# Queries and keys stored transposed and split ahead of each attention, with the value products moved between the two score products, in a two-layer transformer kernel

## The chip, the cores and the metric

The kernel runs on one core of one Trainium2 chip. The metric is device time in microseconds (us) of one execution, the median of three. Lower is better. The engines are TensorE (PE), VectorE (DVE), ScalarE (ACT), GpSimd (POOL) and SyncE (SP, which here only issues DMAs).

## The reference

```python
# x: 4 batches x 1024 tokens x 256 features, 16 heads of 16 features
x = x + ln(attn0(ln(x)))        # attn0: no mask, scores / sqrt(256)
x = x + ln(moe0(ln(x)))         # two loops of a routed MLP, 8 experts of 512
x = x + ln(attn1(ln(x)))        # attn1: causal, ALiBi slopes, biases on q, k, v, scores / sqrt(16)
x = moe1(x)                     # balanced assignment, 8 experts of 1024 (layer norm, gelu, residual)

def attn(x):
    q, k, v = split(x @ w_qkv (+ b_qkv))                # per head 16 features
    s = q @ k.T / scale (+ slope * (key_pos - query_pos), masked above the diagonal)
    return (softmax(s) @ v) @ w_out (+ b_out)
```

All of it is float32 and the output has to match to float32-like accuracy.

## The kernel before

The program is one sequence of stages, each with its own on-chip memory, its own semaphores and a barrier of all engines at its end: `ln_qkv` (layer norm and q, k, v), `attention` without mask, `attn_post`, twice `rms_logits`/`route`/`experts`, `combine_qkv` (the second layer's q, k, v), causal `attention`, `attn_post`, `assigned_experts`. Every engine has its own in-order instruction stream; semaphores tie them.

**The q, k, v stages.** `ln_qkv` and `combine_qkv` walk over 32 tiles of 128 tokens. For each tile TensorE transposes the normalised tokens (`turn`), then computes 768 outputs per token with the tokens on the partitions (`product`: a 512-wide and a 256-wide part, two contraction steps each; `combine_qkv` adds the bias by one more matmul per part). ScalarE copies the 768 columns out of PSUM (`y_out`) and stores them with one DMA of 384 KB in pieces of 64 floats, grouped by four heads (`qkv`).

**Attention.** It works on 32 pairs of heads. In `raw` lie the q, k, v of four heads with tokens on the partitions. A float32 number is split into a high part (rounded to what one fast `float32r` pass takes exactly) and the rest; q and k become rows of 64 columns per head: 5 columns for the row maximum and the positions, then 16 high, 16 high or rest, 16 rest or high. GpSimd builds these rows (`natural`), TensorE turns them (`fill`: four 128x128 transposes into the PSUM bank `TP`, four fills for a pair), ScalarE copies each half into `qT` or `kT` (`evac`). A `fill` and the transposes of the output (`finish`) share that bank, and the waits `t_bank_read` order them.

A pair is processed twice over: first the natural scores (queries on the partitions), of which VectorE takes the row maxima (`scores`, `rowmax`), then the transposed scores with the maximum subtracted (`qk`), of which ScalarE takes the exponential (`exp`), whose result goes into the value product (`pv`, four column groups for two steps at once). The maxima of one pair run beside the exponentials of the pair before. One pair is a *slot* of NS steps: 16 without mask, 12 with it. Each step issues, on TensorE in this order, `qk(n)`, then the natural scores of the step (`scores`, called m(n) below: the unit `max_at(n)`, four units ahead), then in odd steps `pv`. All scores live in a ring of three PSUM buffers (`s_free`), in the order e(0), m(0), e(1), m(1), ...; so `qk(n)` waits until VectorE has finished the maxima of step n-2, and `scores` of step n waits until ScalarE has finished `exp(n-1)`:

```python
ring={}
for n in range(NS):
    ring["e",n]=len(ring)%3
    if max_at(n)[0] is not None: ring["m",max_at(n)[0]]=len(ring)%3
    if n==TURN: ring["t",0]=len(ring)%3
```

At `TURN` (step 12, or 8 with the mask) the maxima of a pair are complete: VectorE reduces them (`mfinal`), TensorE turns them, VectorE copies them (`mcopy`) and SP writes them as one row of `qT` (`place`), which `qk(0)` of the next slot awaits. At step 4 and again at step 12 (without the mask) `finish` turns the output of one half and VectorE sums and scales it (`add`, `scale`).

The SP stream of attention: the loads of the first heads, in the first attention then the weights for the MLP stages (`ahead`), then the loop with loads, `place`, `store`.

## Time and profile before

| | us |
|---|---|
| three runs | 3403.23, 3406.68, 3409.97; median 3406.68 |
| the profiled execution, its own time | 3403.33 |
| span of its trace, first to last instruction | 3401.6 |

| stretch of the span | us | what runs there |
|---|---|---|
| 0 to 108 | 108 | `ln_qkv` |
| 108 to 1015 | 907 | attention without mask, begin of `attn_post` |
| 1015 to 1990 | 975 | `attn_post`, MLP of the first layer |
| 1990 to 2130 | 140 | `combine_qkv` |
| 2130 to 2815 | 685 | causal attention |
| 2815 to 3401 | 586 | `attn_post`, MLP of the second layer |

Busy shares over the span: PE 80%, DVE 58%, ACT 48%, POOL 28%. How to read it: a wait only costs where it lies on the chain that sets the end of its stage, so each stage has to be read by itself, in the timeline of its engines.

### The profile page before, as it was taken

The page shows a single profiled execution, that of the slowest core. Times are in us where ns is not written, and L with a number is a line of the kernel's source. Part 1 is how long each engine was busy: PE and PEld are TensorE (multiplying, and loading weights), DVE is VectorE, ACT ScalarE, POOL GpSimd, SP SyncE. Part 2 cuts the span into 40 slices and gives each one's busy share as a digit, 9 for nine tenths or more (in the row PEclk, how much of TensorE's full clock was granted, in tenths as well). Part 3 has the DMA queues.
Part 4 walks back from the last instruction along what each step waited for, and adds up shares of the span by engine and source line. Part 5 has one row for each costly group of instructions (what it writes and reads, how often), then busy time and mean ns, then how long its engine had stood idle before and what let it go on. Part 6 is the DMA issues. An engine that isn't in the chain of part 4 may idle for free. (4 is left out here: it accounts for less than half of the span.)

```text
span 3401.6 us, 63393 instructions
## 1 busy us (share of the span) xinstructions
PE 2729.3 (80%) x16332; PEld 1619.0 (48%) x16333; DVE 1966.6 (58%) x4600; ACT 1625.9 (48%) x2553; POOL 959.6 (28%) x1653
## 2 busy tenths in 40 slices
PE   8699999999977449995399959688888887718887
PEld 5333333333324438874388724344444444415554
DVE  3488888888845353335533354576667754556641
ACT  3277777777754433333333334366666663302212
POOL 1411111111126115541155444322222213403333
PEclk9699999999995569995599979799999996759999
DMA  6501010010013102214022166111111104322331
GB/s 168 168 20 24 14 25 19 19 25 13 19 40 113 56 16 69 68 58 149 14 69 68 59 174 183 44 26 25 31 26 30 25 10 121 119 92 70 99 100 61
DMA packets 365685, 215.08 MB, mean 63 GB/s; under 512 B 284782, under 2 KB 345842, under 8 KB 364791
## 3 DMA queue, kind: packets, MB, share of 16 engines
q1 hardware_dynamic: 231224, 106.71, 11.8%
q10 hardware_dynamic: 116416, 54.53, 5.5%
q0 software_dynamic: 17920, 52.46, 4.9%
q8 instruction: 43, 0.70, 0.1%
q14 instruction: 82, 0.67, 0.1%
HBM read 129.20 MB, written 85.98 MB: 63 GB/s over the span
## 5 line engine op out<-in xcount | busy, mean ns | idle before, releaser
L339 ACT ACTIVATE att_pr<-att_S 128x1024 f32<-128x1024 f32 (+1 forms) x896 | 836.1, 941 | 427.5 <-ACTq L346 424.4
L379 DVE TENSOR_REDUCE att_mparts<-att_S 128x2 f32<-128x1024 f32 x640 | 777.1, 1225 | 169.1 <-DVEq L375 165.2
L255 PE MATMUL att_S<-att_qT,att_kT 64*128 64x512 f32 (+3 forms) x1792 | 430.0, 472 | 46.4 <-PEq L250 42.1
L271 PE MATMUL att_OP<-att_pr,att_vn 128*32 128x512 f32 (+3 forms) x3584 | 451.1, 564 | 1.0 <-PEq L265 0.7
L243 PE MATMUL att_S<-att_kT,att_qT 64*128 64x512 f32 (+3 forms) x1792 | 391.0, 430 | 74.1 <-PEq L237 62.7
L255 PEld LDWEIGHTS att_S<-att_qT,att_kT 64*128 64x128 f32 x1792 | 175.0, 184 | 471.9 <-issue 460.7
L179 POOL COPY att_vn<-att_raw 128x256 f32<-128x256 f32 x64 | 25.4, 396 | 1148.6 <-POOLq L178 1148.6
L243 PEld LDWEIGHTS att_S<-att_kT,att_qT 64*128 64x128 f32 x1792 | 188.0, 190 | 173.0 <-issue 167.1
L385 DVE CUSTOM_DVE_ANT_0 att_unused<-att_S,att_mask 128x128 f32<-128x128 f32 (+3 forms) x512 | 228.3, 488 | 69.9 <-DVEq L375 69.9
L1067 POOL DMA_INDIRECT experts_xs<-scaled,ffn_source x144 | 140.2, 974 | 353.2 <-SPq L1060 163.5
L1164 DVE COPY experts_y<-experts_Y 128x256 f32<-128x256 f32 x144 | 61.2, 425 | 223.3 <-DVEq L1163 223.3
L1138 ACT ACTIVATE experts_hh<-experts_TH 128x512 fp32r<-128x512 f32 x144 | 86.2, 598 | 204.2 <-ACTq L1137 202.7
L1073 POOL DMA_INDIRECT mixed<-experts_y,ffn_target x144 | 146.2, 1016 | 92.5 <-issue 43.1
L1161 DVE TENSOR_TENSOR experts_hl<-experts_TH,experts_hh 128x512 fp32r<-128x512 f32 x144 | 99.6, 692 | 111.8 <-DVEq L1159 111.0
L1141 ACT ACTIVATE experts_h<-experts_H 128x512 f32<-128x512 f32 x144 | 86.2, 599 | 127.5 <-ACTq L1140 127.5
L1406 PE MATMUL ffn_Y<-ffn_w,ffn_hT 128*128 128x256 f32 x512 | 128.5, 402 | 8.9 <-PEq L1405 8.9
L1401 PE MATMUL ffn_H<-ffn_xT,ffn_w 128*128 128x512 f32 x256 | 121.1, 630 | 13.4 <-PEq L1399 9.1
L479 POOL TENSOR_TENSOR post_s<-post_s,post_half 128x2 f32<-128x2 f32 x128 | 97.1, 758 | 115.3 <-POOLq L651 109.1
L675 PE MATMUL post_Y<-post_w,post_aT 128*128 128x256 f32 x256 | 107.2, 563 | 27.8 <-PEq L673 27.8
L271 PEld LDWEIGHTS att_OP<-att_pr,att_vn 128*32 128x32 f32 x3584 | 72.0, 108 | 109.7 <-issue 105.3
L336 ACT ACTIVATE att_qT<-att_TP 128x512 fp32r<-128x512 f32 x128 | 76.1, 594 | 90.5 <-ACTq L334 90.5
L1406 PEld LDWEIGHTS ffn_Y<-ffn_w,ffn_hT 128*128 128x128 f32 x512 | 97.1, 198 | 33.7 <-issue 20.8
(291 smaller groups left out, 4913.0 us busy)
## 6 DMA issues: line engine op xcount, KB each, us to landing
qkv<-qkv_y ACTq DMA_DIRECT2D x64, 384.0 KB, 3.4
att_raw<-qkv SPq DMA_DIRECT2D x96, 256.0 KB, 3.3
rows<-post_rows ACTq DMA_DIRECT2D x32, 384.0 KB, 2.7
ffn_w<-in_w ACTq DMA_DIRECT2D x12, 1024.0 KB
ao<-att_aon SPq DMA_DIRECT2D x32, 256.0 KB, 2.8
post_at<-ao SPq DMA_DIRECT2D x64, 128.0 KB, 3.1
scaled<-rms_zs SPq DMA_DIRECT2D x64, 128.0 KB, 1.7
rms_rows<-mixed SPq DMA_DIRECT2D x32, 256.0 KB, 3.6
```

The costliest lines, as they stand in the source:

```text
L243: mm=pe.matmul(S[:,b,h,at:at+n],qT[r,s,qt*128:qt*128+128],kT[r,s,half*512:half*512+n],start=True,stop=True)
L255: mm=pe.matmul(S[:,b,h,f:512],kT[r,s,kt*128:kt*128+128],qT[r,s,c*512+f:c*512+512],start=True,stop=not diag)
L271: mm=pe.matmul(OP[32*j:32*j+32,f:512],vn[:,s,kt,h,:],pr[:,n%4,h,f:512],start=kt<2,stop=g in last_groups,skip_group_check=True)
L339: nc.scalar.activation(pr[:,n%4,:,f:512],S[:,ring["e",n],:,f:512],ACT.Exp,scale=exp_scale).then_inc(s_free[ring["e",n]],1)
L379: nc.vector.tensor_reduce(mparts[:,s,:,2*qt+half],S[:,b,:,0:width(qt,half)],AX.X,ALU.max).then_inc(end,1)
L385: nc.vector.tensor_tensor_reduce(unused[:,2*i+h,0:n],S[:,b,h,at:at+n],mask[:,512-n:512],1.0,-3.0e38,ALU.add,ALU.max,mparts[:,s,h,2*qt+half ...
L675: mm=pe.matmul(Y[:,u%4,0:DIM],aT[:,u%2,128*k:128*k+128],w[:,k,:],start=k==0,stop=k==KC-1 and not last)
L1067: nc.gpsimd.indirect_dma_start(out=xs[:,t%R,:],out_offset=None,in_=zs_d,in_offset=bass.IndirectOffsetOnAxis(ap=source[:,t:t+1],axis=0)).th ...
L1073: nc.gpsimd.indirect_dma_start(out=y2_d,out_offset=bass.IndirectOffsetOnAxis(ap=target[:,t:t+1],axis=0),in_=y[:,t%RY,:],in_offset=None, bo ...
L1161: V.tensor_tensor(hl[:,u%2],TH[:,u%2,:],hh[:,u%2].bitcast(F32),ALU.subtract).then_inc(hT_ready,1)
L1401: mm=pe.matmul(H[:,c%2,:],w1[:,e%2,k,128*c:128*c+128],xT[:,k,:],start=k==0,stop=k==KC-1)
L1406: if c<FC: pe.matmul(Y[:,t%2,0:DIM],hT[:,c,128*t:128*t+128],w2[:,e%2,c,:],start=c==0,stop=False)
```

## The change

Queries and keys are no longer stored with tokens on the partitions. `ln_qkv` and `combine_qkv` compute them with the features on the partitions (`features`: one block of 128 features by 512 tokens per step), ScalarE writes the high part (`high`, with the bias in the second layer), VectorE the rest (`low`), and SP stores both parts (`keep_block`, 512 KB); v is computed and stored alone (`values`, `v_out`, `keep_v`, 128 KB). The stages' steps are delayed against each other by whole tiles (`lagged`), and the loops over the tiles are written out. In attention, `natural`, `fill`, `evac` and the identity in `float32r` are gone; SP loads the parts into the rows of `qT` and `kT` directly, 14 or 16 DMAs of at most 64 KB per pair, into four sets instead of two. The constant rows are cleared or set at the start, for `kT` on VectorE. In a step, TensorE now issues `qk(n)`, in odd steps `pv`, then the natural scores.

```diff
 # attention, SP
+                def load_set(b,pair):
+                    s=pair%SETS; done=set_loaded[s]
+                    sp.wait_ge(set_free,1).then_inc(set_free,-1)
+                    for m,T,high,both in ((0,qT,AUG,AUG+HD),(1,kT,AUG+2*HD,AUG)):
+                        for h in range(2):
+                            to=lambda row,n: T[64*h+row:64*h+row+n,s,:].bitcast(F32)
+                            parts=qk_d[m][:,bass.ds(b*HEADS+2*pair+h,1)].bitcast(F32)
+                            sp.dma_start(to(high,HD),parts[0,0]).then_inc(done,16)
+                            for x in range(2): sp.dma_start(to(both+HD*x,HD),parts[x,0]).then_inc(done,16)
+                            if causal: sp.dma_start(to(0,AUG),augr[...,m,:].bitcast(F32)).then_inc(done,16)
+                            elif m==0: sp.dma_start(to(0,1),zeros[:].bitcast(F32)).then_inc(done,16)
+                def during(b,c,first,last):
+                    if not (last and c+3>=COUPLES): load_set(*later(c+3))
+                    if c%2==0: ...   # store of the group before, load_v of the next
+                    if not (last and c+1>=COUPLES): place(c+1)
+                for c in range(3): load_set(0,c)
+                load_v(0,0)
                 if ahead:
                     for k in range(KC): sp.dma_start(w1[:,k,:].bitcast(F32),...).then_inc(w_loaded[k],16)
...
+                place(0)
 # attention, GpSimd: natural() is removed, values() stays
+                pool.wait_ge(keys_cleared,2+causal).then_inc(keys_cleared,-2-causal)
+                pool.sem_inc(set_free,SETS); pool.sem_inc(rv_free,1)
 # attention, TensorE
                     for n in range(NS):
                         if e is not None: qk(e,n)
                         x,ahead=max_at(n)
-                        if m is not None and n==0: t_bank_read()
-                        if a is not None and n==NS-EARLY: t_bank_read()
                         s=a if ahead else m
                         unit=x is not None and s is not None
+                        g=(n-2)//2 if n>1 else GROUPS_PV-1
+                        who=prev if n<2 else e
+                        if who is not None and n%2==1:
+                            if g in (0,CHUNK0): o_ready(g,e,prev)
+                            pv(who,g)
                         if unit: scores(s,x)
                         if m is not None and n==TURN: turn_max()
-                        if m is not None and n==0: fill(m,0,1)
-                        ...   # four fills in all, removed
-                        g=(n-2)//2 if n>1 else GROUPS_PV-1
-                        who=prev if n<2 else e
-                        if who is not None:
-                            if n%2==0 and not unit: exp_read(2*g+1)
-                            if n%2==1:
-                                if g in (0,CHUNK0): o_ready(g,e,prev)
-                                pv(who,g)
+                        if prev is not None and n==2: pe.sem_inc(set_free,1)
+                        if who is not None and n%2==0 and not unit: exp_read(2*g+1)
                         if prev is not None and n==4: finish()
-                        if e is not None and n==KEYS0+1: finish()
+                        if e is not None and n==ADD0: finish()     # ADD0=NS-EARLY
 # attention, ScalarE: evac() and its four calls per slot are removed
 # attention, VectorE
+                nc.vector.memset(kT[:].bitcast(F32),0.0).then_inc(dve_done,1)     # 128 x 4*1024
                 nc.vector.memset(mparts[:],-3.0e38).then_inc(dve_done,1)
+                for h in range(2): nc.vector.memset(kT[64*h:64*h+1].bitcast(F32),-1.0).then_inc(keys_cleared,1)
                 if causal:
+                    nc.vector.tensor_copy(augr[:],augf[:]).then_inc(keys_cleared,1)   # 80 x 2048
 # ln_qkv (combine_qkv likewise, with its bias and longer lags)
+def lagged(stages):
+    for n in range(NT+max(lag for lag,stage in stages)):
+        for lag,stage in stages:
+            if 0<=n-lag<NT: stage(n-lag)
+                lagged(((0,load),(11,keep_v),(15,keep_block)))      # SP; combine_qkv: keep_v 14, keep_block 18
+                def features(q):                                    # TensorE
+                    f=q%4
+                    pe.wait_ge(q_free,1).then_inc(q_free,-1)
+                    for k in range(KC):
+                        mm=pe.matmul(Q[:,q%4],w[:,k,128*f:128*f+128],xT[:,k,q//4%2,:],start=k==0,stop=k==KC-1)
+                    mm.then_inc(q_full,1)
+                lagged(((5,values),(3,turn),(8,features)))          # combine_qkv: 8, 6, 11
+                def high(q):                                        # ScalarE
+                    act.wait_ge(q_full,1)...; act.wait_ge(hl_stored[q%HB],16)...
+                    nc.scalar.activation(hl[:,q%HB,0],Q[:,q%4],ACT.Copy).then_inc(high_ready,1)
+                lagged(((9,high),(4,turned),(7,v_given),(6,v_out)))
+                def low(q):                                         # VectorE
+                    dve.wait_ge(high_ready,1).then_inc(high_ready,-1)
+                    done(nc.vector.tensor_tensor(hl[:,q%HB,1],Q[:,q%4],hl[:,q%HB,0].bitcast(F32),ALU.subtract))
+                    dve.sem_inc(q_free,1); dve.sem_inc(low_ready,1)
+                lagged(((2,normal),(0,x_stats),(10,low)))
```

In `combine_qkv` the bias of q and k goes into `high` and `low`; v keeps its bias matmul, 256 wide. The outputs of the two layouts are the same numbers.

## Rows read from the trace of the kernel before

**Rows 1.** Stretches: length, busy us by engine, granted clock, DMA share, GB/s

```profile
108.00:1015.00 907.00, 790.56 (x4918) 318.42 (x4918) 686.31 (x779) 612.66 (x711) 160.82 (x313) 0.96 0.12 32
...
2130.00:2815.00 685.00, 583.08 (x4896) 315.87 (x4896) 457.07 (x1410) 405.74 (x576) 141.49 (x356) 0.97 0.12 26
```

**Rows 2.** Timeline, first attention: start, duration, engine, line, operation, idle before

```profile
525.45 0.49 PE L255 MATMUL att_S<-att_qT,att_kT 64*128 64x512 f32 x2
...
526.08 1.03 ACT L339 ACTIVATE att_pr<-att_S 128x1024 f32<-128x1024 f32 x1 [0.39 <-ACTq L346]
...
527.25 0.50 PE L243 MATMUL att_S<-att_kT,att_qT 64*128 64x512 f32 x2
...
527.68 1.06 PE L271 MATMUL att_OP<-att_pr,att_vn 128*32 128x512 f32 x8
527.90 1.23 DVE L379 TENSOR_REDUCE att_mparts<-att_S 128x2 f32<-128x1024 f32 x1 [0.18 <-DVEq L375]
...
528.67 0.50 PE L255 MATMUL att_S<-att_qT,att_kT 64*128 64x512 f32 x2
```

**Rows 3.** Timeline, first attention: transposed scores released by a maximum

```profile
508.31 1.23 DVE L379 TENSOR_REDUCE att_mparts<-att_S 128x2 f32<-128x1024 f32 x1
...
509.68 0.50 PE L255 MATMUL att_S<-att_qT,att_kT 64*128 64x512 f32 x2 [0.18 <-PEq L250]
```

**Rows 4.** Timeline, first attention: m(11), and `qk(13)` behind the turn

```profile
517.11 0.49 PE L243 MATMUL att_S<-att_kT,att_qT 64*128 64x512 f32 x2 [0.26 <-PEq L237]
...
520.38 0.50 PE L255 MATMUL att_S<-att_qT,att_kT 64*128 64x512 f32 x2
```

**Rows 5.** Timeline, causal attention: two turns, and the output transposes between them

```profile
2403.84 0.27 PE L285 MATMUL att_S<-att_ident,att_m 128*16 128x128 f32 x1
...
2418.36 0.63 PE L279 MATMUL att_TP<-att_ident,att_ot 128*128 128x128 f32 x4 [1.08 <-PEq L221]
...
2423.97 0.27 PE L285 MATMUL att_S<-att_ident,att_m 128*16 128x128 f32 x1 [0.15 <-PEq L284]
```

**Rows 6.** Timeline, start of the first attention

```profile
109.20 1.80 POOL L147 MEMSET att_qn<- 128x2048 f32 x1 [16.87 <-POOLq L29]
...
116.14 1.38 SPq L135 DMA_DIRECT2D ffn_w<-in_w  x2
...
126.74 0.80 PE L243 MATMUL att_S<-att_kT,att_qT 64*128 64x512 f32 x2 [1.02 <-PEq L237]
...
135.31 5.72 SPq L114 DMA_DIRECT2D att_raw<-qkv  x2
...
149.33 1.49 SPq L121 DMA_DIRECT2D att_qT<-att_mT  x2
...
152.50 0.79 PE L255 MATMUL att_S<-att_qT,att_kT 64*128 64x512 f32 x2 [0.82 <-PEq L250]
```

**Rows 7.** Timeline, start of the causal attention: two DMA issues of SP

```profile
2131.92 1.01 SPq L114 DMA_DIRECT2D att_raw<-qkv  x2
```

**Rows 8.** Instructions on `qkv_y`: min/median/max ns, first and last start

```profile
L599 ACT ACTIVATE qkv_y<-qkv_Y x32: 811/811/812, 16.7 to 104.0; 128x768 f32<-128x768 f32 x32
...
L1259 ACT ACTIVATE qkv_y<-qkv_Y x32: 811/812/812, 2001.0 to 2121.6; 128x768 f32<-128x768 f32 x32
```

**Rows 9.** Stretches of `ln_qkv`, weight loading and `combine_qkv`, columns as in Rows 1

```profile
20.00:40.00 20.00, 20.00 (x71) 11.87 (x70) 8.54 (x29) 8.55 (x15) 3.84 (x7) 1.00 0.77 187
...
116.00:126.00 10.00, 1.45 (x8) 1.13 (x8) 0.00 (x0) 0.75 (x2) 6.08 (x15) 0.50 1.12 378
...
2020.00:2040.00 20.00, 20.00 (x64) 9.91 (x64) 12.70 (x37) 11.03 (x21) 12.52 (x32) 1.00 0.94 239
```

**Rows 10.** Timeline, `ln_qkv`: the statistics of two tiles in a row

```profile
9.32 0.43 DVE L538 BATCH_NORM_STATS2 qkv_st<-qkv_xt 128x6 f32<-128x256 f32 x1 [0.44 <-DVEq L553]
...
11.34 0.43 DVE L538 BATCH_NORM_STATS2 qkv_st<-qkv_xt 128x6 f32<-128x256 f32 x1 [0.44 <-DVEq L553]
```

**Rows 11.** Groups by line: a 512-wide split on VectorE

```profile
L1161 DVE TENSOR_TENSOR experts_hl<-experts_TH,experts_hh 128x512 fp32r<-128x512 f32 x144 | 99.6, 692 | 111.8 <-DVEq L1159 111.0 <-ACT experts_hh L1138 0.7
```

More of the change, by code:

```diff
@@ L285, in turn_max, with slot, set_of @@
                     pe.transpose(S[0:2*TILES,b,0,0:128],m16[:],ident[:]).then_inc(mt_full,1)
-                def slot(e,prev,m,after):
-                    a=None if not after else 1-m
+                def slot(j,first,count):
+                    def set_of(ahead): return (j+ahead)%SETS if 0<=first+j+ahead<count else None
+                    e,prev,m,a=set_of(0),set_of(-1),set_of(1),set_of(2)
                     for n in range(NS):
@@ L604, in _, with v_out @@
-                pipelined(act,[turned,y_out])
-                if bias is None:
-                    for i in range(2): act.wait_ge(stored[i],16)
+                    nc.scalar.activation(xT[:,:,t//4%2,128*(t%4):128*(t%4)+128],T[:,t%2,0:DIM].rearrange("p (k c) -> p k c",k=KC),ACT.Copy).then_inc(xT_ready,1)
+                def v_out(t):
+                    act.wait_ge(v_full,1).then_inc(v_full,-1); act.wait_ge(v_stored[t%2],16).then_inc(v_stored[t%2],-16)
+                    nc.scalar.activation(v[:,t%2],V[:,t%2,0:DIM],ACT.Copy).then_inc(v_done,1)
@@ L608, in attn_post @@
+                for i in range(HB): act.wait_ge(hl_stored[i],16)
 def attn_post(nc,tag,ao,w_d,x_in,ident_d,x_out=None,z=None,bias_d=None,g_d=None,b_d=None,cent_d=None,rows_d=None,scores=None):
@@ L1277, in _ @@
-                done(V.tensor_copy(high[:],bias[:]))
-                done(V.tensor_tensor(low[:],bias[:],high[:].bitcast(F32),ALU.subtract))
-                done(V.tensor_scalar(low[:],low[:],ident[0:2,1:2],None,ALU.mult))
-                done(V.scalar_tensor_tensor(out=biasr[:],in0=high[:].bitcast(F32),scalar=ident[0:2,0:1],in1=low[:],op0=ALU.mult,op1=ALU.add))
+                done(V_.memset(ones[:].bitcast(F32),1.0))
+                done(V_.tensor_copy(split[:],bias[:]))
+                done(V_.tensor_tensor(rest[:],bias[:],split[:].bitcast(F32),ALU.subtract))
@@ L1281, in _ @@
+                done(V_.tensor_scalar(rest[:],rest[:],ident[0:2,1:2],None,ALU.mult))
+                done(V_.scalar_tensor_tensor(out=biasr[:],in0=split[:].bitcast(F32),scalar=ident[0:2,0:1],in1=rest[:],op0=ALU.mult,op1=ALU.add))
                 dve.sem_inc(bias_ready,1)
                 dve.sem_inc(rows_free,RR)
-                def weighted(s,b,u):
-                    V.scalar_tensor_tensor(out=row(z,b,u),in0=rows[:,u%RR,s],scalar=weight[:,s,bass.ds(b*TILES+u,1)],in1=row(z,b,u),op0=ALU.mult,op1=ALU.add).then_inc(dve_done,1)
```

496 lines of the change are left out of this document (204 added, 292 removed).

## The prediction

> **What bounds the kernel now.** I read the stretches first, then the timeline inside each stage that the change touches, because the busy shares alone don't say which wait ends last. The two attentions take 907 and 685 us of the span [rows 1]; PE is busy 87% and 85% of them, DVE 76% and 67%, ACT about 60%, and the granted clock is 0.96 and 0.97, that is 2.4 GHz nearly throughout. No engine is full, so the chain through them counts.
>
> In the first attention it closes every two steps [rows 2]. I write qk(n) for the transposed scores, m(n) for the natural scores of the same step. With the start of qk(even) at 525.45, its exponential starts at 526.08 (0.63 later) and takes 1.03; then m(odd) may overwrite that buffer, at 527.25 (0.14 after the end); `pv` follows at 527.68 (0.43); the next qk(even) starts at 528.67 (0.99). The sum is 0.63+1.03+0.14+0.43+0.99 = 3.22 us, and 528.67-525.45 is 3.22. The reader is to see that `pv` stands inside this loop, that the fills and ScalarE's copies mostly stand beside it, and that m(odd) waits for an exponential while PE idles.
>
> A second loop lies just beneath. m(odd) at 527.25 starts its maximum at 527.90 (0.65), which takes 1.23 and releases qk of the odd step after: 509.68 is 0.14 after the end of the maximum that began at 508.31 [rows 3]. From there to m(odd) another 0.43 or less: 0.65+1.23+0.14+0.4 = 2.4, hidden under 3.22 as long as `pv` is not in it.
>
> **The first attention.** The reorder takes `pv` out of the first loop and puts it into the second. PE's order becomes qk(even), m(even), qk(odd), pv, m(odd). qk(odd) still has to wait for the maximum of the last m(odd), `pv` is behind it in the queue, and m(odd) behind `pv`. The new loop is m(odd) to its maximum 0.65, maximum 1.23, release 0.14 [rows 3], qk(odd) to `pv` 0.43 (from m(odd) to `pv` now, the same shape), `pv` to m(odd) 0.99 (from `pv` to qk now): 3.44 us in place of 3.22. The old chain, without `pv`, is no longer the bound: exp(even) ends while `pv` runs. VectorE does its even maximum and the sums of the output (under 1 us at steps 4 and 12) inside the 3.44, which has room for 3.44-2x1.23 = 0.98.
>
> One pair of steps differs, where the row maxima are turned. From m(11) at 517.11 to qk(13) at 520.38 is 3.27 [rows 4], set by maximum, final reduce, turn and `finish`, none of which changes. Then m(13) comes 0.43+0.99 = 1.42 behind qk(13): 4.69. A slot is 7x3.44+4.69 = 28.8 us. For the slot before I take 7x3.22, and 3.27 plus 0.41 for m(13) directly behind qk(13), which is 26.2, and the stray 0.3 that the fills and copies add: 26.5 (from qk(0) at 152.50 [rows 6] to 1015, less some 13 for the last output and the next stage's start, over 32 slots, gives 26.5 too). So +2.3 per slot; the removal of fills and copies is already in it, worth only those 0.3. 32 slots x 2.2 (to stay with measured links) = **+71 us**. If every link were 0.05 shorter it would be +10, if VectorE lost its slack at steps 4 and 12 another +20.
>
> **The causal attention.** A slot is 20.13 us (2423.97-2403.84 [rows 5]) and VectorE runs nearly without a break. Two things pull. `finish` at 2418.36 waited 1.08 us for the shared bank that a fill held; that goes, and VectorE gets its sum about 0.5 us earlier. Against it, between m(1) and m(3) lie two full-width maxima, so the loop of 3.44 holds there while VectorE has only 2.46 of work: it idles 0.98. Between the other odd steps the maxima are narrow or masked and `pv` of the diagonal is shorter; following the same links I find 0.1 us lost before m(1) and 0.4 at step 9. The sum is -0.5-0.2+0.98+0.1+0.4 = +0.8 per slot, x32 = **+26 us** (bounds -0.5 and +2 per slot: -16 and +64).
>
> **Starts of the attentions.** No DMA of q and k may start before `kT` is cleared on VectorE: 128x4096, then twice one row of 4096. The trace has no such memset on VectorE; the nearest is 128x2048 on POOL, 1.80 us [rows 6], so 3.6 each and 10.8 for three, with 0 (if one row is cheap) to 21 as bounds. The Trainium skill (VectorE: DVE Perf Modes, "Zero memsets can be issued as uint32") says a memset takes one cycle per element, an estimate of 4.3 us each at 0.96 GHz, 12.8 for three; that would add 2 us per attention to the sum; no run here shows it yet. Then 14 DMAs at 0.5 us of issue each (1.01 for two [rows 7]) and some 2.3 to land (1.7 from the end of `place`'s issue to qk(0) [rows 6] is the nearest row): first natural scores at 109.2+10.8+7+2.3 = 129.3 instead of 126.74 [rows 6]. The larger delay is `place(0)`. SP now issues the loads of three pairs (42x0.5 = 21 us, until 141), then the weights, which took it from 116.14 to 135.31, 19.2 us [rows 6], and only then `place(0)`, at 161. Now it is issued at 149.33 and qk(0) starts 3.17 later, at 152.50 [rows 6]. So qk(0) at 164: **+11.5 us**. The causal attention has no such weights; with 10.8 of memsets, 1.8 for the position rows (2048 wide, by the same row), 8 of issue and 2.3 it starts its scores about **+5 us** later. GpSimd's building of rows, most of its 161 us in 907 [rows 1], goes too, from beside the path; its own waits hide it.
>
> **The q, k, v stages.** `ln_qkv` runs at (104.0-16.7)/31 = 2.82 us per tile, `combine_qkv` at 120.6/31 = 3.89 [rows 8], PE busy all of the time [rows 9]. PE's work in `ln_qkv` stays: as many columns, 1536 per tile. VectorE at its own pace took 2.02 per tile [rows 10]; `low` adds 0.69 [rows 11] and its waits, about 0.25: 2.97, now above PE's 2.82. The first ten steps run at 2.02, so only some 22 tiles pay 0.15 (+3), and the delayed steps leave a tail of five feature blocks and two value tiles, 10 us, before the last split is stored, where PE also idled at the start: about +1. Sum **+4 us**. In `combine_qkv` the 512-wide bias matmul goes. What that stage has over the other is 1.07 per tile for 768 columns of bias; two thirds would be 0.71, nothing is the other bound, and I take 0.43, what 512 columns take before `pv` [rows 2]: PE 3.46; VectorE, busy 12.70 of 20 us [rows 9], so 2.46 per tile, plus waits 0.4 and `low` 0.69: 3.6. That is -0.25 per tile, and a longer tail of 3: **-5 us**. DMA: per tile 640 KB are stored in pieces of 1 and 2 KB instead of 384 KB in pieces of 256 bytes. `ln_qkv` would move 0.79 MB per 2.97 us, 265 GB/s; `combine_qkv` 1.18 MB per 3.6, 328. The trace has 187 GB/s at a DMA share of 0.77 and 239 at 0.94, 243 to 254 at a full share, with 256-byte pieces, and 378 at 1.12, 337, with large ones [rows 9]. At the lower rate the stages would take 3.2 and 4.6 per tile, +8 and +24 us more; at the upper it hides. I take the upper, since the pieces are long.
>
> **Sum**, against the execution's own 3403.33 (span 3401.6): +71+26+11.5+5+4-5 = +112, so 3516; the median of the runs is 3.4 us above the profiled one, so **3519**.
>
> **Rivals.** (A) *The released loop wins, the time falls.* If qk(odd) doesn't wait for the odd maximum in practice, because that maximum starts early enough, what is left is VectorE's own work: 16x1.23 = 19.7, 1.7 of reduces and sums (686.31/32 less 19.7 [rows 1]) and as much again of waits, 23.2 per slot, -3.3x32 = -106 us in the first attention and -0.5x32 = -16 in the second, with +20 for starts and stages: 3305. It decides from the point where maximum plus release plus the link to `pv` is under 1.4 us instead of the 1.8 that rows 2 and 3 give. For it: DVE is idle a quarter of the time [rows 1] and PE idles before m(odd). Against: 0.14 at 509.68 is a wait on exactly that maximum [rows 3]. 13%. (B) *The loops even out*: the 0.22 is made up by links that shorten and by the missing fills; only starts and stages stay: 3403+16 to +40, 3430. 17%. (C) *The clock falls.* PE's work per two steps is four score pairs of at most 0.43 and `pv` 0.99, 2.7 of 3.44 us (79%), against the same and the fills in 3.22 (84% and more) [rows 2]. At the start of the attention, with maxima alone, the clock was at its lower level: the same pair of matmuls took 0.80 [rows 6] instead of 0.50 [rows 2]. Were it so in a third of the slots, the links 0.43 and 0.99 would double there, +1.42 per two steps, 11x8x1.42 = +125 over the forecast: 3645. The Trainium skill (TensorE: Matmul & The Clock Gate, the section on the transpose mode) says transposes don't count as busy the same way; by it the fills that go never held the clock, which makes C less likely; nothing here shows it apart. 6%. (D) *DMA-bound stages* on top of the forecast: +32, 3551; inside the forecast's range.
>
> **Numbers.** Forecast (with D) 64%, own range 3475 to 3575. Rival A 13%, B 17%, C 6%. The range of 8 in 10 has to reach into B: 3412 to 3585. What a measurement can tell from no change is about 0.2%, 7 us. Faster 0.15 (A, and a little of B), within 0.2% 0.03, slower 0.82.
>
> **What would show it.** Right: in the first attention the transposed scores of odd steps start 0.14 after a maximum, `pv` follows at 0.43, m(odd) 0.99 after; two steps take 3.44, a slot near 28.8; VectorE has a gap of about 1 us before each odd maximum; ScalarE's copies are gone and its waits have grown by more than that; qk(0) of the first attention starts some 11 us later behind the weights' issues. Wrong: VectorE's maxima back to back, a slot under 26.5, or `pv` starting before the maximum is done; a clock below 0.9 in the attentions; q, k, v stages over 3.2 and 4 us per tile with a DMA share near 1.

## The result, and the profile after

The changed kernel takes 3622.17 us (median of 4 runs, 3614.42 to 3628.47), the one before 3408.32 in the same runs: ratio 1.0628, 95% interval 1.0603 to 1.0653. The direction was as forecast, the size was twice as large: +214 instead of +112, above the range. The profiled execution has a span of 3626.7 us, 225.1 more than before, and they lie here (from first and last starts in the two traces; a stage begins with its first DMA issue, "steps" runs from the first qk to the last one of an attention):

| stretch | before | after | measured | forecast |
|---|---|---|---|---|
| `ln_qkv`, up to the first attention's start | 109.2 | 135.6 | +26.4 | +4 |
| first attention, start to qk(0) | 43.3 | 62.1 | +18.8 | +11.5 |
| first attention, steps | 840.4 | 950.0 | +109.6 | +71 |
| last qk to the causal attention's start | 1134.0 | 1157.4 | +23.4 | -5 |
| causal attention, start to qk(0) | 38.8 | 46.1 | +7.3 | +5 |
| causal attention, steps | 643.5 | 678.4 | +34.9 | +26 |
| rest | 592.4 | 597.1 | +4.7 | 0 |

`combine_qkv` alone grew by 23.7, from 162.5 to 186.2 us. The stretches of the changed kernel, in the columns of [rows 1]: they are longer by 129 and 42 us, PE's work is smaller, VectorE's is within 8 us of what it was, and the granted clock is 0.91 and 0.92 instead of 0.96 and 0.97.

```profile
134.00:1170.00 1036.00, 717.14 (x4406) 275.55 (x4406) 685.57 (x780) 565.11 (x582) 46.02 (x55) 0.91 0.16 45
2308.00:3035.00 727.00, 553.80 (x4384) 286.68 (x4384) 464.19 (x1414) 343.69 (x448) 14.38 (x35) 0.92 0.20 52
```

The timeline of the first attention, which answers [rows 2, 3] (L221 transposed scores, L209 natural scores, L237 `pv`, L325 maxima):

```profile
573.31 0.49 PE L221 MATMUL att_S<-att_qT,att_kT 64*128 64x512 f32 x2 [1.06 <-PEq L216]
573.73 1.07 PE L237 MATMUL att_OP<-att_pr,att_vn 128*32 128x512 f32 x8
...
574.73 0.50 PE L209 MATMUL att_S<-att_kT,att_qT 64*128 64x512 f32 x2
...
575.38 2.36 DVE L325 TENSOR_REDUCE att_mparts<-att_S 128x2 f32<-128x1024 f32 x2 [1.09 <-DVEq L321]
...
576.75 0.49 PE L221 MATMUL att_S<-att_qT,att_kT 64*128 64x512 f32 x2 [1.06 <-PEq L216]
```

This is the forecast loop, link by link: 0.42, 1.00, 0.65, then 1.37 for the maximum and its release; 3.44 us from 573.31 to 576.75. PE waits 1.06 and VectorE 1.09 in each round.

The turn, a few microseconds later, was not in the forecast (L250 the transposition of the maxima, L245 the output transposes):

```profile
578.17 0.50 PE L209 MATMUL att_S<-att_kT,att_qT 64*128 64x512 f32 x2
...
578.75 0.39 PE L209 MATMUL att_S<-att_kT,att_qT 64*128 64x512 f32 x2
580.77 0.27 PE L250 MATMUL att_S<-att_ident,att_m 128*16 128x128 f32 x1 [1.64 <-PEq L249]
580.93 0.63 PE L245 MATMUL att_TP<-att_ident,att_ot 128*128 128x128 f32 x4
581.48 0.80 PE L221 MATMUL att_S<-att_qT,att_kT 64*128 64x512 f32 x2
582.21 1.93 PE L237 MATMUL att_OP<-att_pr,att_vn 128*32 128x512 f32 x8
584.07 0.79 PE L209 MATMUL att_S<-att_kT,att_qT 64*128 64x512 f32 x2
```

PE has been idle for 1.64 us, and behind it the same products take 0.80, 1.93 and 0.79 instead of 0.49, 1.07 and 0.50: the granted clock has gone from 2.4 to 1.2 GHz. Before, PE waited 0.45 us ahead of the turn (median of 31 turns; now 1.64). The record of the granted clock has 24 stretches at the lower level in the steps of the first attention, 107 us in all; before there was one, of 10 us, right at their beginning.

`ln_qkv` (L522 the value product, L515 the transposition, L528 a feature block, L544 ScalarE's copy of it):

```profile
69.69 0.60 ACT L544 ACTIVATE qkv_hl<-qkv_Q 128x512 fp32r<-128x512 f32 x1 [2.48 <-ACTq L543]
...
70.06 1.10 PE L522 MATMUL qkv_V<-qkv_w,qkv_xT 128*128 128x256 f32 x4 [0.59 <-PEq L520]
...
71.00 0.38 PE L515 MATMUL qkv_T<-qkv_ident,qkv_xn 128*128 128x128 f32 x2
71.22 1.88 PE L528 MATMUL qkv_Q<-qkv_xT,qkv_w 128*128 128x512 f32 x4
...
73.32 0.60 ACT L544 ACTIVATE qkv_hl<-qkv_Q 128x512 fp32r<-128x512 f32 x1 [2.48 <-ACTq L543]
...
73.69 1.10 PE L522 MATMUL qkv_V<-qkv_w,qkv_xT 128*128 128x256 f32 x4 [0.59 <-PEq L520]
```

A step takes 3.63 us (forecast 2.97). PE waits 0.59 in these, at L520, the wait for a free bank of values, while ScalarE itself waits 2.48. In `combine_qkv` most steps take 4.41, and PE waits 0.91 at the same place.

The start of the first attention, which answers [rows 6]:

```profile
136.55 3.47 DVE L309 MEMSET att_kT<- 128x4096 f32 x1 [6.43 <-PEq L29]
...
141.12 3.47 DVE L312 MEMSET att_kT<- 1x4096 f32 x1 [1.02 <-DVEq L311]
...
145.50 3.47 DVE L312 MEMSET att_kT<- 1x4096 f32 x1 [0.91 <-issue]
...
180.62 0.27 DVE L354 CAST att_mT<-att_S 16x128 fp32r<-16x128 f32 x1
...
190.22 1.49 SPq L127 DMA_DIRECT2D att_qT<-att_mT  x2
...
197.72 0.80 PE L221 MATMUL att_S<-att_qT,att_kT 64*128 64x512 f32 x2 [15.22 <-PEq L216]
```

One memset takes 3.47 us, a memset of one row as long as that of the whole tile (forecast 3.6, from the row of GpSimd). The 4.3 estimated from the Trainium skill (VectorE: DVE Perf Modes, "Zero memsets can be issued as uint32") was too long for one; the measurement decides. But the three with the waits between them took 12.4 us, from 136.55 to 148.97. The maxima are ready at 180.9, but their placing waits in SP's queue until 190.22 behind the weights, and it now takes 6.0 us from the end of its issue to qk(0), not 1.7.

### The profile page after: what moved, and what is told of

It is laid out like the page before. It is cut to its first block and busy times, and to the rows that moved or that the text cites. A ratio compares the mean times of both kernels' runs of the same rounds, so it can differ in the third digit from the quotient of the medians.

```text
span 3626.7 us, 61395 instructions
## 1 busy us (share of the span) xinstructions
PE 2617.5 (72%) x15276; PEld 1537.2 (42%) x15277; DVE 2015.4 (56%) x4669; ACT 1518.0 (42%) x2361; POOL 716.3 (20%) x1074
## 5 line engine op out<-in xcount | busy, mean ns | idle before, releaser
L325 DVE TENSOR_REDUCE att_mparts<-att_S 128x2 f32<-128x1024 f32 x640 | 765.0, 1222 | 337.8 <-DVEq L321 336.4
L221 PE MATMUL att_S<-att_qT,att_kT 64*128 64x512 f32 (+3 forms) x1792 | 411.8, 448 | 348.9 <-PEq L216 346.5
L237 PE MATMUL att_OP<-att_pr,att_vn 128*32 128x512 f32 (+3 forms) x3584 | 484.5, 603 | 0.9 <-PEq L231 0.7
L209 PE MATMUL att_S<-att_kT,att_qT 64*128 64x512 f32 (+3 forms) x1792 | 411.4, 459 | 85.2 <-PEq L203 83.9
L221 PEld LDWEIGHTS att_S<-att_qT,att_kT 64*128 64x128 f32 x1792 | 192.1, 194 | 550.4 <-issue 547.1
L209 PEld LDWEIGHTS att_S<-att_kT,att_qT 64*128 64x128 f32 x1792 | 189.2, 199 | 456.9 <-issue 440.8
L1108 DVE COPY experts_y<-experts_Y 128x256 f32<-128x256 f32 x144 | 61.1, 425 | 225.1 <-DVEq L1107 225.1
L237 PEld LDWEIGHTS att_OP<-att_pr,att_vn 128*32 128x32 f32 x3584 | 72.9, 110 | 95.5 <-issue 84.3
L1033 PE MATMUL experts_H<-ffn_w1h,experts_xh 128*128 x288 | 104.7, 445 | 4.0 <-PEq L1041 3.1
```

Source lines behind the costliest of these rows:

```text
L209: mm=pe.matmul(S[:,b,h,at:at+n],qT[r,s,qt*128:qt*128+128],kT[r,s,half*512:half*512+n],start=True,stop=True)
L221: mm=pe.matmul(S[:,b,h,f:512],kT[r,s,kt*128:kt*128+128],qT[r,s,c*512+f:c*512+512],start=True,stop=not diag)
L237: mm=pe.matmul(OP[32*j:32*j+32,f:512],vn[:,s%2,kt,h,:],pr[:,n%4,h,f:512],start=kt<2,stop=g in last_groups,skip_group_check=True)
L325: nc.vector.tensor_reduce(mparts[:,s,:,2*qt+half],S[:,b,:,0:width(qt,half)],AX.X,ALU.max).then_inc(end,1)
L1033: mm=pe.matmul(out,a[:,128*k:128*k+128],b[:,k,bass.ds(at,width)],start=start and n==0 and k==0,stop=stop and n==len(pairs)-1 and k==chunks-1)
```

## The experiments

Each kernel ran in 3 rounds beside the kernel before, whose median was 3403.32 us for e1 to e4, 3408.19 for e5 to e8 and 3403.32 for e9 to e12. Stretches as in the table above, one profiled execution each; "low" is the time at the lower clock within the steps of an attention, of which 4 to 23 us at the head of each stand in every kernel. "Slot" runs from one transposition of the maxima to the next: the mean of the slots that ran wholly at the higher clock, and in brackets how many of the 30 had some time at the lower one. The edits are shown shortened.

| kernel | us | ln | start 1 | steps 1 | mid | start 2 | steps 2 | low 1 | low 2 | slot 1 | slot 2 |
|---|---|---|---|---|---|---|---|---|---|---|---|
| before | 3408.3 | 109.2 | 43.3 | 840.4 | 1134.0 | 38.8 | 643.5 | 10 | 7 | 26.52 (0) | 20.37 (1) |
| after | 3622.2 | 135.6 | 62.1 | 950.0 | 1157.4 | 46.1 | 678.4 | 107 | 70 | 28.92 (22) | 20.84 (13) |
| e1_pv_back | 3465.7 | 135.7 | 62.5 | 838.8 | 1153.3 | 46.1 | 625.1 | 13 | 30 | 26.44 (0) | 19.52 (7) |
| e2_before_pv_moved | 3517.8 | 109.9 | 43.4 | 927.7 | 1132.3 | 38.8 | 671.7 | 48 | 11 | 28.87 (11) | 21.20 (0) |
| e3_pv_early | 3529.8 | 135.5 | 61.8 | 875.8 | 1155.2 | 46.0 | 660.1 | 11 | 39 | 27.42 (0) | 20.41 (1) |
| e4_given_first | 3576.9 | 117.8 | 62.1 | 946.9 | 1127.0 | 46.1 | 686.5 | 101 | 98 | 29.00 (18) | 20.88 (16) |
| e5_pv_halves | 3479.2 | 135.4 | 62.3 | 821.0 | 1154.5 | 46.1 | 665.4 | 37 | 118 | 24.97 (5) | 19.93 (16) |
| e6_finish_first | 3589.6 | 135.9 | 62.0 | 907.3 | 1157.3 | 46.0 | 690.3 | 21 | 119 | 28.58 (0) | 20.77 (16) |
| e7_gap_filled | 3661.5 | 136.1 | 62.6 | 919.9 | 1161.1 | 46.1 | 735.8 | 8 | 92 | 29.08 (0) | 22.17 (21) |
| e8_starts | 3603.7 | 135.9 | 40.5 | 946.0 | 1160.4 | 41.2 | 687.3 | 94 | 107 | 28.98 (20) | 20.79 (17) |
| e9_mixed | 3384.9 | 117.7 | 40.6 | 827.7 | 1124.1 | 40.5 | 636.9 | 45 | 76 | 24.98 (6) | 19.45 (18) |
| e10_all_back | 3402.5 | 117.6 | 40.5 | 841.4 | 1125.3 | 41.2 | 642.9 | 12 | 100 | 26.45 (1) | 19.36 (26) |
| e11_before_halves | 3437.9 | 109.8 | 43.3 | 874.4 | 1128.1 | 38.8 | 643.2 | 4 | 10 | 27.61 (0) | 20.33 (0) |
| e12_gap_transposes | 3594.0 | 135.7 | 62.3 | 913.4 | 1152.3 | 46.0 | 694.1 | 9 | 129 | 28.90 (0) | 20.80 (17) |

In the changed kernel the slots of the first attention without a fall of the clock take 28.92 us and the 22 with one 30.50, so that the falls cost 22x1.58 = 35 us there. In the causal one it is 20.84 and 22.22: 13x1.38 = 18 us. The slots without a fall are the steadier measure: kernels with the same order in an attention agree in them to 0.2 us.

### The place of `pv`

**e1_pv_back**, on the changed kernel:

```diff
                         qk(e,n)
-                        if who is not None and n%2==1: pv(who,g)
                         if unit: scores(s,x)
+                        if who is not None and n%2==1: pv(who,g)
```

> The changed kernel with one edit: pv stands behind the natural scores again, as before. Theory (pv in the loop of the maxima costs 3.45 instead of 3.22 us per two steps, and the longer idle gap of PE at each turn lets the granted clock fall to its lower level, about 1 us per slot): the stretch from the first to the last qk of the first attention falls from 950 to 840-855 us (before: 840.4), the causal one from 678 to 640-650, the clock holds at the turns, two steps take 3.22 us; the time is 3622-105-35 = 3480 us, and the +26 of ln_qkv, +23 of combine_qkv and +26 of the two starts stay. Rival 1 (the clock falls because the fills are gone from the slot, not because of the order): the dips stay, the first attention at 880 us, the time near 3520. Rival 2 (sets of four, delayed steps and fewer transposes cost, not the place of pv): no more than 40 us come back, 3580 or more.

3465.69 us, ratio to before 1.019 (1.0167 to 1.0213). 156 us come back (168 between the two profiled executions), 111 in the first attention and 53 in the causal one, where some 30 to 40 were expected: both rivals are out. The steps are now shorter than before the change (838.8 and 625.1 against 840.4 and 643.5). So what else the change does to the steps, fills and copies dropped and `finish` moved, was by itself a gain of 2 and 18 us.

**e2_before_pv_moved**: the opposite edit on the kernel before, `pv` moved between the two scores and nothing else.

> The kernel before with one edit: pv between the transposed and the natural scores, as in the change; fills, copies and everything else as before. Theory: two steps take 3.45 us, the first attention +70 us, the causal one +25; if the clock then falls at the turns too, +38 more. 3408+95 = 3503 without dips, 3540 with them. Rival (the fills stood in PE's wait and closed the gap): the clock holds and it is 3503; rival 2 (the order costs nothing by itself): 3415 or less.

3517.82 us, ratio 1.033 (1.0313 to 1.0347). This lies between the two times expected, with and without falls of the clock. The move alone costs 87 and 28 us. The clock falls less often (11 slots instead of 22), with the fills still in the slot and a wait of 1.17 us ahead of the turn instead of 1.64. The move is the cause in either structure, and what it adds in slots without a fall, 2.35 and 0.83 us, or 75 and 27 in 32, is close to the bare loop term (+71 and +26).

**e3_pv_early**: `pv` one step earlier, behind the natural scores of the even step.

```diff
-                        if who is not None and n%2==1: pv(who,g)
                         if unit: scores(s,x)
+                        if who is not None and n%2==0:
+                            if not unit or n not in covered: exp_read(2*g+1)
+                            pv(who,g)
```

> The changed kernel with one edit: pv of a group is issued right behind the natural scores of the even step, one step earlier (those scores have already waited for its exponential; where they do not, a wait for it stands ahead). Theory: pv then stands neither between the exponential and m(odd) nor between a maximum and m(odd), where it delays the next link; it fills the time in which PE waits for exp(even). Two steps then take PE's own work, 4 pairs at 0.43 and pv 0.99 with small gaps, 2.8 us, VectorE 2.46: a slot of 24.3 us instead of 30, the first attention 750-770 instead of 950, the causal one 620-650 instead of 678, clock near 1; the time 3622-190-40 = 3390. Rival (PE's queue or the maxima bind anyway: qk(odd) behind pv is late, and with it exp(odd)): two steps at 3.2, the first attention 860, the time 3500.

3529.81 us, ratio 1.0364 (1.0345 to 1.0383): my theory (3390) fell, the rival (3500) was near. The timeline of this kernel (L223 transposed, L211 natural scores, L239 `pv`, L292 exponentials; the line of L292 covers two in a row, the first of 1.02):

```profile
566.46 0.50 PE L211 MATMUL att_S<-att_kT,att_qT 64*128 64x512 f32 x2 [0.83 <-PEq L205]
...
566.89 1.07 PE L239 MATMUL att_OP<-att_pr,att_vn 128*32 128x512 f32 x8
...
567.89 0.50 PE L223 MATMUL att_S<-att_qT,att_kT 64*128 64x512 f32 x2
...
568.52 1.94 ACT L292 ACTIVATE att_pr<-att_S 128x1024 f32<-128x1024 f32 x2 [1.28 <-ACTq L298]
...
569.68 0.49 PE L211 MATMUL att_S<-att_kT,att_qT 64*128 64x512 f32 x2 [0.42 <-PEq L205]
```

Two chains run side by side, one through each exponential: natural scores, next transposed scores, exponential (0.63+1.02+0.14), natural scores two steps on. A whole `pv` lengthens whichever of the two it stands in: 569.68-566.46 = 3.22, the loop of [rows 2] on the other parity. The slot is still 1.0 us longer than in e1 (27.42 against 26.44); where that lies was not taken apart.

**e5_pv_halves**: half of the columns in each.

```diff
+                        if who is not None and n%2==0: ...; pv(who,g,0,256)
+                        if who is not None and n%2==1: pv(who,g,256,512)
```

> The changed kernel with pv in two halves of 256 columns: the first behind the natural scores of the even step 2g+2, the second behind those of the odd step. The run with pv early had shown 3.2 us per two steps, since a pv between m(even) and qk(odd) stands in the loop of the other exponential. Theory (each of the two chains exp -> natural scores -> pv part -> next transposed scores then carries 0.5 us of pv instead of 0 and 1.0): 0.63+1.03+0.14+0.43+0.5 = 2.73 us, and PE's own work of 2.8-2.9 binds: a slot of 23.7 to 24.5 us, the first attention 755-780 us instead of 950, the causal one 600-625 instead of 678, no dips of the clock; 3622-180-65 = 3375. Rival (a half costs as much as the whole in each step, because the loads of weights and the pipeline bind, or VectorE's maxima bind at 3.1): the first attention 840 or more, 3465.

3479.17 us, ratio 1.0214 (1.0185 to 1.0243). A half takes 0.57 to the next scores, and two steps 2.91 us:

```profile
568.22 0.51 PE L223 MATMUL att_S<-att_qT,att_kT 64*128 64x512 f32 x2
568.56 0.41 PE L211 MATMUL att_S<-att_kT,att_qT 64*128 64x512 f32 x2
...
568.90 0.64 PE L239 MATMUL att_OP<-att_pr,att_vn 128*32 128x256 f32 x8
569.47 0.50 PE L223 MATMUL att_S<-att_qT,att_kT 64*128 64x512 f32 x2
570.02 0.61 PE L211 MATMUL att_S<-att_kT,att_qT 64*128 64x512 f32 x2
...
570.56 0.64 PE L239 MATMUL att_OP<-att_pr,att_vn 128*32 128x256 f32 x8
...
571.13 0.50 PE L223 MATMUL att_S<-att_qT,att_kT 64*128 64x512 f32 x2
```

A slot without a fall takes 24.97 instead of 26.44 with the whole `pv` in its old place, 47 us in 32. The first attention gains only 18 of them, since the clock now falls in 5 slots, and those take 30.29. The causal attention loses 40, with 118 us low against 30, and 0.4 us more in a slot without a fall. In this kernel both halves open their accumulation, so that its sums lack products of the first half; its instructions and their order are those meant.

### The clock at the turn

**e6_finish_first** and **e7_gap_filled**, on the changed kernel:

```diff
# e6
+                        if e is not None and n==ADD0: finish()
                         if m is not None and n==TURN: turn_max()
-                        if e is not None and n==ADD0: finish()
# e7
+    for t in range(8): pe.matmul(TP[...],ident[:],ident[:],start=True,stop=True)
                         if m is not None and n==TURN: turn_max()
```

> The changed kernel with one edit: at the turn, the output transposes (finish) stand ahead of the transposition of the maxima, in the 1.64 us in which PE waits for it, instead of behind. Theory (that gap is what lets the granted clock fall at the turn, about 70 us at the lower level in 775): the gap shrinks to about 1 us, the dips go, and finish leaves the path (0.64 per slot): the first attention 950-20-35 = 895 us, the causal one 678-10-10 = 658, 3622-75 = 3547. Rival (the clock falls for the idle time of the whole loop, not for the gap): only 0.64 per slot, the first attention 930, 3590, and the dips stay.

> The changed kernel with eight extra 128x128 products into the bank of the output transposes, put ahead of the wait for the maxima at each turn: about 1.3 us of work that nothing needs, in the gap of 1.64 us; no other order changes. Theory (the gap lets the clock fall): no dips, the first attention 950-35 = 915 us, the causal one 668, 3622-45 = 3577, although PE has more to do. Rival (the dips come from the 1.06 us of idle time in every two steps): dips as before or fewer, the time the same within 10 us or longer by what of the extra work is not hidden, 3622 or more.

e6: 3589.64 us, 1.0523 (1.05 to 1.0546); e7: 3661.52 us, 1.0742 (1.0724 to 1.076). **e12_gap_transposes** is e7 with transposes in place of the products, in the first attention alone:

> The changed kernel with eight 128x128 transposes in the gap at the turn, in the first attention alone, where eight products of the same size took the dips of the granted clock away (first attention 950 to 920 us). Theory 1 (transposes count as little as the Trainium skill, TensorE: Matmul & The Clock Gate, says of the transpose mode): the dips stay and the first attention stays near 950 us, the time 3622. Theory 2 (any work of PE in the gap holds the clock, as the run with the output transposes moved into it suggests, 907 us and no dips): no dips, 920 us, 3592.

3594.01 us, 1.0557 (1.0539 to 1.0574). Stretches 300 to 900 us, in the first attention, columns as in [rows 1], of the changed kernel, e6, e7 and e12, one fence each:

```profile
300.00:900.00 600.00, 434.48 (x2740) 166.35 (x2740) 420.56 (x482) 351.69 (x361) 8.01 (x20) 0.95 0.14 36
```
```profile
300.00:900.00 600.00, 432.75 (x2887) 168.50 (x2885) 441.05 (x505) 369.66 (x379) 8.46 (x21) 1.00 0.15 37
```
```profile
300.00:900.00 600.00, 459.84 (x3167) 203.91 (x3165) 433.85 (x496) 362.90 (x372) 8.06 (x20) 1.00 0.14 36
```
```profile
300.00:900.00 600.00, 445.50 (x3013) 184.43 (x3013) 436.36 (x499) 365.51 (x375) 8.40 (x21) 1.00 0.14 36
```

In all three the granted clock goes from 0.95 to 1.00 and more of VectorE's work fits into the same 600 us. In e12 the gap ahead of the turn is 0.62 instead of 1.64 us, with nothing of the kernel's own moved:

```profile
566.63 1.09 PE L244 MATMUL att_TP<-att_ident 128*128 128x128 f32 x8
568.35 0.27 PE L253 MATMUL att_S<-att_ident,att_m 128*16 128x128 f32 x1 [0.62 <-PEq L252]
568.46 0.60 PE L248 MATMUL att_TP<-att_ident,att_ot 128*128 128x128 f32 x4
568.99 0.51 PE L221 MATMUL att_S<-att_qT,att_kT 64*128 64x512 f32 x2
```

The steps go from 950.0 to 913.4 us (e12) and 919.9 (e7), though PE has more to do: the falls of the clock at the turn cost some 37 us there, and the slots of the changed kernel that had no fall are as long as those of e12 (28.92 and 28.90). e6 gave 43: the falls, and 0.34 us per slot for `finish` instead of the 0.64 expected. The 1.06 us of waiting in every round, which stays, doesn't cause them alone. Useless transposes held the clock as well as useless products. The Trainium skill (TensorE: Matmul & The Clock Gate, on the transpose mode) says that a transpose "doesn't count as PE-busy the same way"; no effect of that is seen here, and the measurement decides.

In the causal attention the edits failed: 70 us low in the changed kernel, 119 and 92 in e6 and e7, and e7 lost 57 us, so that both kernels missed their times. The traces show why: there PE waits 0.10 us ahead of the turn (median), so that there was no gap to fill, and the products of e7 stood in PE's way (22.17 us per slot against 20.84). Nearly all falls come at another place, 17 to 20 us behind a turn. The changed kernel has a wait of some 1.2 us there in nearly every slot, for a maximum. In this slot the scores behind it run at the lower clock, and the turn (L250) then comes without a wait:

```profile
2447.83 0.50 PE L221 MATMUL att_S<-att_qT,att_kT 64*128 64x512 f32 x2 [1.22 <-PEq L216]
...
2449.92 0.80 PE L221 MATMUL att_S<-att_qT,att_kT 64*128 64x512 f32 x2
...
2451.18 0.38 PE L250 MATMUL att_S<-att_ident,att_m 128*16 128x128 f32 x1
```

No kernel here filled that wait. In e12, where that attention is left as it was, there were 129 us low and 16 us more, with the same 20.80 us in a slot without a fall: how often the clock falls there varies between kernels in which that attention is the same.

### The q, k, v stages and the starts

**e4_given_first**, on the changed kernel, and likewise in `combine_qkv`:

```diff
-                lagged(((9,high),(4,turned),(7,v_given),(6,v_out)))
+                lagged(((7,v_given),(9,high),(4,turned),(6,v_out)))
```

> The changed kernel with one edit in both q, k, v stages: ScalarE gives the bank of the value product back at the beginning of its step, ahead of the copy of the features. Theory (a cycle of PE and ScalarE: the value product waits for a release that stands behind the copy of features issued last on PE): ln_qkv goes from 3.63 to about 3.0 us per tile (-20), combine_qkv from 4.12 to 3.7 (-13): 3590. Rival (these stages are bound by the longer transfers, or by VectorE's split): less than 5 us, 3620.

3576.86 us, 1.0495 (1.047 to 1.0519): -18 in `ln_qkv` and -30 up to the causal attention. The step of `ln_qkv`:

```profile
69.79 1.03 PE L522 MATMUL qkv_V<-qkv_w,qkv_xT 128*128 128x256 f32 x4
...
71.24 1.88 PE L528 MATMUL qkv_Q<-qkv_xT,qkv_w 128*128 128x512 f32 x4
...
72.95 1.03 PE L522 MATMUL qkv_V<-qkv_w,qkv_xT 128*128 128x256 f32 x4
```

3.16 instead of 3.63, and PE no longer waits before the value product. In the first part of the stage a step even takes 2.80, PE's own work; the 3.16 come later, where PE waits 0.17 us or more for the normalised tokens ahead of their transposition. In `combine_qkv` most steps take 3.26 instead of 4.41. Only the place of one release on ScalarE changed, so transfers and VectorE's splits were not the bound; 8.6 us are left in `ln_qkv`, and `combine_qkv` takes 157.5 us, 5 less than before (forecast +4 and -5).

**e8_starts**, on the changed kernel:

```diff
-                place(0)            # behind the weights
+                place(0)            # ahead of them
-                memset(kT[:],0.0); for h in range(2): memset(kT[64*h:64*h+1],-1.0)
+                memset(kT[:],-1.0)
```

> The changed kernel with two edits at the starts of the attentions: kT is set to -1 by one memset instead of to 0 and then two rows to -1 (its unused rows meet zeros of qT), and the placing of the first maxima is issued ahead of the weights. Theory: the first natural scores start 8.9 us earlier in both attentions (14.3 and 16.5 us after the start of the stage instead of 23.2 and 25.4), and qk(0) of the first attention 10 more, 43 us after the start of the stage instead of 62.1; the causal one 37 instead of 46.1: 3622-28 = 3594. Rival (GpSimd's own memsets of 5.5 us, or the loads, bind anyway; the weights issued later delay the second placing by up to 10 us): 3610.

3603.72 us, 1.0558 (1.0528 to 1.0588). The starts shrink by 21.6 and 4.9 us: the first natural scores come 8.2 us earlier in the first attention and 4.9 in the causal one, where I expected 8.9, and qk(0) another 13 in the first. The weights issued later delayed nothing that shows. Of these 26 us 18 are left in the time; the causal steps took 9 more, with 107 us low against 70.

### Put together

**e9_mixed**: halves in the first attention, `pv` behind the natural scores in the causal one, e4 and e8. **e10_all_back**: the same with the whole `pv` behind the natural scores in both. **e11_before_halves**: the kernel before with halves in the first attention.

```diff
# e9, e11: only the first half opens the accumulation
-  pe.matmul(OP[...,f:z],...,start=kt<2,...)
+  pe.matmul(OP[...,f:z],...,start=kt<2 and a==0,...)
```

> The changed kernel with all that the runs point to: pv in halves of 256 columns in the first attention, pv behind the natural scores in the causal one, the release of the value bank first on ScalarE, one memset of kT and the placing ahead of the weights. In the run with halves both halves opened their accumulation, which was wrong: opening the second also cleared what marks the first as written; here only the first opens. Theory (the parts add up from the single runs): first attention 821, causal 625, ln_qkv 118, combine_qkv 30 us less, starts 40.5 and 41: 3622-129-53-47-26 = 3367 us, 1.2% below the kernel before. Rival (the parts share slack, above all the clock: the denser stages lose what they gain in dips): 3400 or more.

> As the run before, but pv whole and behind the natural scores in both attentions. Theory: the first attention 839 instead of 821, all else as there: 3385 us, 0.7% below the kernel before; that is then what the change gives with its move of pv left out and the two stages and starts mended. Rival (the splits and transfers of the new stages cost more than the fills they replace): 3410 or more.

> The kernel before with one edit: pv in halves of 256 columns in the first attention, one behind the natural scores of each step; fills and copies stay. Theory (two loops of 2.9 us instead of one of 3.2; but fills and ScalarE's copies fall into the time that was idle): the first attention 815 to 825 instead of 840: 3390. Rival (with the fills PE has no room: 0.57 for a half, twice, is 0.15 more than the whole): 840, 3408; PE as the bound would even give 845.

e9: 3384.94 us (3378.45 to 3390.05), ratio 0.9945 (0.9928 to 0.9961), faster than both kernels, by 0.55% (small, but clear of the interval) and 6.4%, but 18 us short of the sum of its parts: 7 and 12 in the steps. e10: 3402.54, ratio 1.000 (0.9989 to 1.0011), 17 short, in the causal steps: the same code took 642.9 us there with 100 us low, and 625.1 with 30 in e1. In both kernels the clock took what is missing there, as the rival of e9 said: a slot without a fall is no longer than in e5 and e1 (24.98, and 19.45 and 19.36), but 18 and 26 slots of the causal attention had a fall instead of 7, and 6 of the first one in e9 instead of 5. e11: 3437.89, 1.011 (1.0093 to 1.0126), a miss: I expected a gain, and the rival's price was too small as well. Its stretch 300 to 900 beside the same of the kernel before:

```profile
300.00:900.00 600.00, 548.56 (x4722) 237.16 (x4722) 463.62 (x523) 411.46 (x478) 83.97 (x189) 1.00 0.09 20
```
```profile
300.00:900.00 600.00, 546.57 (x3469) 218.78 (x3471) 482.38 (x544) 430.44 (x499) 87.85 (x198) 1.00 0.09 20
```

PE is busy 91% in both, but e11 gets 523 of VectorE's instructions done and before 544. A slot grew from 26.52 to 27.61 us, by as much as the eight pairs of halves add to PE's work (8x0.14 = 1.1, from 2x0.57 against 1.00). That fits PE's own work as what sets the slot with fills and halves; PE still waits 9% of the time, and no run removed the fills alone. The same halves gain where the fills are gone (827.7 in e9 against 841.4 in e10). That is what the change buys: room on PE, which only counts once `pv` is off the single chain.

## Why the prediction was right and wrong

The time was forecast 102 us too short, or 113 between the profiled executions. Of the 113, 51 lie in the q, k, v stages, 48 in the attentions, 10 in their starts and 5 in the rest.

- **q, k, v stages: the step that failed most, +4 and -5 against +26.4 and +23.7.** I bounded each engine by its own work and took the larger. I didn't follow the order on ScalarE: the bank of step n-2 is released behind ScalarE's wait for the block of features that PE issued last, so that the value product waits for the end of that block and starts 0.59 us behind it. e4 shows it: with the release first, the stages come within 5 us of the forecast. The stores (rival D) were not the bound: 205 to 228 GB/s at a DMA share of 0.63 to 0.70 is 326 at a full share, near the upper rate that I took. (D itself was summed wrong: 4.6 against the 3.6 forecast would be 32 us in `combine_qkv`, not 24.)
- **Loop of the first attention: right.** Forecast 3.44, measured 3.44, with all four links. +109.6 less the 37 of the clock (e12) leaves 73 for it; the forecast had 71.
- **The step that failed in the first attention is the turn.** I wrote that maximum, final reduce, turn and `finish` don't change. Their durations don't: from m(11) to qk(13) it takes 3.31 us, forecast 3.27. But PE's wait ahead of the turn became 1.64 us, and the granted clock fell behind it, so that m(13) comes 2.59 behind qk(13) and not 1.42. Rival C named the clock, asked only for the average busy share, and got 6%; it was neither the forecast nor alone, since it came on top: 37 of the missing 39 us. It had a third of the slots at 11 us each, where 22 of 30 had a fall at 1.6 us.
- **Causal attention: +26 against +34.9, near in part by luck.** Slots without a fall grew from 20.37 to 20.84, 15 us in 32; the rest is the clock, 18 us, which I had put at nothing. The 15 are a difference of two terms, both near mine: the move of `pv`, +1.32 us per slot (20.84 against 19.52 in e1; I had 1.48), and the rest of the change to the steps, -0.85 (I had -0.7). On the kernel before the move gave +0.83 (e2). That VectorE runs there nearly without a break was misread: it is busy 67% [rows 1].
- **Starts: right mechanism, mis-sized, +18.8 and +7.3 against +11.5 and +5.** `place(0)` came at 190.22, 54.6 us after the stage began; I had 161-109.2 = 51.8. The first load of q was issued 13.8 us after the stage began instead of 10.8, since the memsets begin late and wait 0.9 to 1.0 us between each other. What I left out is behind the placing: the next pair's loads, issued at once, and 6.0 us instead of 1.7 from its issue to qk(0), the links that I took over from before unchanged. Whether those loads caused the longer landing was not tried by itself. In the causal one the first scores came 25.4 us after the start, where my terms give 22.9; its first load was issued at 14.9 instead of 12.6, which is 2.3 of the 2.5.
- **Rivals A and B: wrong.** The loop through the maxima binds, as [rows 3] said. (ScalarE is busy 68% in the first attention [rows 1], not about 60; nothing hangs on it.)

Open: why the clock falls in some slots of the causal attention and not in others, behind a wait that nearly all of them have: the same code had a fall in 7 of 30 slots in one kernel and in 26 in another. The steps of a single profile differ there by some 20 us for that alone. Also open are the last 8.6 us of `ln_qkv`: later steps wait for the normalised tokens, but why was not tried.

## What to carry to other kernels

When an operation moves within an in-order queue, write down every loop that passes through the queue on each side of it, and add its whole duration to the one it lands in; if each place is in some loop, split it over them. For each buffer release on an in-order engine ask what is queued ahead of it: a release queued behind the copy of the newest product turns two engines that should overlap into one chain. And when a change lengthens a wait of TensorE that comes back in every round, look at the durations behind the wait, not only at the wait; compare rounds with and without a fall of the clock in one trace, which needs no further run.

## What the runs showed of the hardware

- A wait of 1.64 us on TensorE, once in about 30 us, was followed by a granted clock of 1.2 instead of 2.4 GHz in 22 of 30 slots (107 us low in 950); with 1.17 us (e2) in 11. With the wait cut to 1.05 (e6) or 0.62 us (e12) the lower clock was gone from that attention but for its head and one short stretch in e6. Transposes did as well as products. In the causal attention a wait of 1.1 to 1.2 us per slot had falls in 7 of 30 slots in e1 and in 26 in e10, and one of 1.09 in the kernel before had one: these runs give no length from which the clock falls.
- A memset of one partition by 4096 took as long as one of 128 by 4096, 3.47 us.
- With an accumulation opened on each half of a bank's columns (e5), the output was off by a relative 0.14, as if later products of the first half no longer added to what stood there. Opening only the first half (e9, e11) was enough for both.
- Four value products of 256 columns took 0.57 us to the next scores, of 512 columns 1.00: 0.14 us more for two halves than for the whole.
